# Linear attention with a butterfly feed-forward layer: keys of two batches biased by a maximum on VectorE, their sums on GpSimd, first slots and low parts in another order

## Chip, cores and metric

The kernel runs on one core of a Trainium2 chip. The metric is the device time of one execution in microseconds (us); of several runs the median is taken.

## What is computed

The input `x` is 4 batches of 1024 tokens with 128 channels. The layer is post-norm linear attention followed by a post-norm feed-forward layer. Cut to what matters:

```python
q, k, v = split(x @ W_qkv)                     # 16 heads of 64
q = relu(q @ W_f + b_f)
k = relu(k @ W_f + b_f)
kv = einsum('bhnd,bhne->bhde', k, v)
out = einsum('bhnd,bhde->bhne', q, kv)
k_sum = k.sum(axis=2)
normalizer = einsum('bhnd,bhd->bhn', q, k_sum)
out = out / (normalizer[..., None] + 1e-06)
x = layernorm(x + out @ W_out + b_out)
h = butterfly(x @ W_exp + b_exp, up_weights)   # 9 stages over 512 features
h = butterfly(gelu(h + up_bias), down_weights)
x = layernorm(x + h @ W_con + b_con + down_bias)
```

## The kernel before, in words

**Folding.** `W_f` is multiplied into the query and key weights once (`fold_wf`), `W_out` into the value weights (`fold_vo`), and both butterflies into the feed-forward weights: the up one on GpSimd (`up_step`), the down one on VectorE in nine `down_step` calls. Matrices that feed TensorE as fp32r are kept as a high and a low part; one such product is three matmuls (`split`, line 516). ScalarE writes a high part, VectorE subtracts it from the source to get the low part (`lo`, line 960).

**Slots.** All four compute engines run the same loop of 48 slots, each engine with its own instructions in program order. Nothing but semaphores and the order in which the loop's body is written sets the order of work. Up to slot 4 a slot projects two tiles of 128 tokens to keys, later one tile (`k_tiles`, tile s + 4 in slot s, up to slot 27). Batch 2 has the tiles 16 to 23, batch 3 the tiles 24 to 31. From slot 4 on a slot also projects two of the 64 query steps. From slot 10 on VectorE normalises two query steps a slot (`normalise_q`, line 1061), splits them (`qn_lo`), and one slot later TensorE multiplies them by the head maps (`add_attn`).

**Keys.** A key half-tile (128 tokens by 512 columns) is three matmuls and a fourth one, `ones_r` by `bf_rows` (line 568), which adds the bias `b_f`. ScalarE takes it out of its bank with a ReLU (`k_relu`, line 806). VectorE adds each tile to `k_total` (`k_sum`, lines 1029 and 1033), and TensorE multiplies it by `x` into `kx_ps` (`add_kx`, line 588). ScalarE copies `kx_ps` out at the end of a batch (`kx_copy`), and the sum over the tokens is turned into `ksum_cols` by VectorE (`ksum_mask`, line 1039), in slots 6, 14, 22 and 30.

**Shared banks.** Three PSUM banks form a ring (`ring`) for keys, queries, norms and hidden tiles: a bank is written again when the use three places before it has been taken out. One more bank, `desk`, takes all transposes, the key sums and the head maps, one after another (`desk_of`, `take_desk`): the next use waits until the one before has been copied out. A low part that VectorE still has to make from `desk` therefore holds the next transpose on TensorE. The transposed `x` of a batch goes over `desk` in slots 2, 6, 10, 14, 18 and 22, with its low part made a slot later (`xT_lo`). The transposed attention output goes over it in slots 15, 19, 23, ... (`transpose_attn`), in the first half of TensorE's slot, and the feed-forward output in slots 22, 26, 30, 34, ... (`transpose_y`).

**Layer norms.** In slots 15, 19, 23, ... VectorE adds the residual and takes mean and variance (`add_x`), GpSimd computes the reciprocal root (`rstd_of`, lines 492 and 495), and VectorE ends the norm (`layer_norm_end`, line 1079). From slot 22 on the second norm does the same (`residual`).

**SP's queue.** SP issues the large loads in a fixed order. `load_down(8)`, the last coefficients of the down butterfly, stands behind `spread(0)`, which writes the first reciprocals to memory and reads them back spread over the partitions.

## Time and profile before

| what | value |
|---|---|
| median of 3 runs | 353.05 us (352.67 to 353.06) |
| the profiled execution's own time | 351.33 us |
| its span, first to last instruction | 349.4 us |
| TensorE (PE) busy | 321.5 us, 92% of the span |
| VectorE (DVE) busy | 227.2 us, 65% |
| ScalarE (ACT) busy | 165.5 us, 47% |
| GpSimd (POOL) busy | 77.6 us, 22% |
| mean granted TensorE clock | 0.99 |

A busy share is the time in which an engine works on an instruction. Matmuls are pipelined, so what a matmul costs in a dense stretch is the distance from its start to the next one's start, which is shorter than its duration. "PEld" is the weight load, which overlaps the matmuls. Behind a group stands, in brackets, how long its engine was idle just before it and what ended that.

### The profile page before, as it was taken

Reading aid. Unit: us, or ns where it says so; the run is one execution under the profiler, and the core shown is the slowest. Engines: PE = TensorE matmul, PEld = TensorE weight load, DVE = VectorE, ACT = ScalarE, POOL = GpSimd, SP = SyncE. Lnnn points to the kernel's source line nnn. Section 1 sums busy time; section 2 is a strip of 40 time slices with the busy share of each in tenths; the row PEclk is TensorE's granted clock in tenths of the full one; section 3 lists DMA queues with packets and bytes.
Section 4 is the critical chain, followed back from the end, with each engine's and each line's share of the span. In section 5 each row is a group of like instructions: output and inputs, shape, how many; then the busy total and the mean of one; then the engine's idle time right before and its main releaser. Section 6 shows DMA issues by size and latency. Waiting matters only on the chain.

```text
span 349.4 us, 5085 instructions
## 1 busy us (share of the span) xinstructions
PE 321.5 (92%) x1825; PEld 222.5 (64%) x1825; DVE 227.2 (65%) x471; ACT 165.5 (47%) x273; POOL 77.6 (22%) x77
## 2 busy tenths in 40 slices
PE   4998999999799999999999999999999799999870
PEld 3855677766477767677777677577777466455440
DVE  2534999984979577756632876458638826575643
ACT  3532345444446464565564646365656543233340
POOL 4079599950000001101000110011001102111211
PEclk9999999999999999999999999999999999999996
DMA  6992353826502800720081005600370092190021
GB/s 178 289 265 62 120 180 122 258 108 159 144 2 65 181 0 5 175 68 3 6 217 23 0 2 130 144 2 3 89 185 2 4 215 58 45 248 12 0 61 31
DMA packets 25602, 33.73 MB, mean 97 GB/s; under 512 B 4169, under 2 KB 14441, under 8 KB 25577
## 3 DMA queue, kind: packets, MB, share of 16 engines
q1 hardware_dynamic: 25416, 33.38, 36.2%
q8 instruction: 14, 0.23, 0.3%
q14 instruction: 12, 0.09, 0.1%
q10 hardware_dynamic: 160, 0.03, 0.0%
HBM read 31.04 MB, written 2.36 MB: 96 GB/s over the span
## 4 chain that ended last, share of the span: by engine, by line
PE 77%; DVE 10%; DMA 4%; SPq 2%; issue 2%; POOL 2%; ACT 1%; POOLq 0%; DVEq 0%; ACTq 0%
PE ring L516 27%; PE kx_ps L588 14%; PE attn_ps L516 8%; PE ring L684 7%; PE ring L608 4%; PE attn_ps L638 4%; PE desk L525 4%; PE ring L568 4%; DMA x<-_L_ffn_down_weights_dram 2%; PE desk L622 2%; PE desk L597 2%; DVE qn L1061 2%; DMA xs<-in_L_attn_x_dram 2%; DVE stats L1070 1%; SPq L419 1%
## 5 line engine op out<-in xcount | busy, mean ns | idle before, releaser
L813 ACT ACTIVATE q<-ring,bf_col 128x512 f32<-128x512 f32 x64 | 43.9, 689 | 51.9 <-PE ring L516 51.4
L588 PE MATMUL kx_ps<-k,xs 128*128 128x512 f32 x128 | 60.2, 592 | 0.8 <-ACT k L806 0.8
L492 POOL TENSOR_TENSOR var_eps<-mean_var,ln_eps 128x4 f32<-128x4 f32 x16 | 7.5, 467 | 235.0 <-DVE mean_var L1074 235.0
L806 ACT ACTIVATE k<-ring 128x512 f32<-128x512 f32 x64 | 38.3, 599 | 32.6 <-PE ring L568 32.4
L1061 DVE TENSOR_TENSOR qn<-q,recips 128x512 f32<-128x512 f32 x64 | 42.2, 698 | 3.3 <-DMA recips<-recip_rows 3.3
L960 DVE TENSOR_TENSOR qn_l<-qn,qn_h 128x512 fp32r<-128x512 f32 x48 | 32.1, 680 | 15.2 <-ACT qn_h L799 15.1
L484 POOL TENSOR_TENSOR y<-hid,y_up 128x512 f32<-128x512 f32 x18 | 34.5, 1941 | 20.0 <-DMA hid<-in_L_ffn_up_weights_dram 19.2
L799 ACT ACTIVATE qn_h<-qn 128x512 fp32r<-128x512 f32 x48 | 29.6, 628 | 17.0 <-DVE qn L1061 17.0
L588 PEld LDWEIGHTS kx_ps<-k,xs 128*128 128x128 f32 x128 | 24.1, 189 | 19.2 <-issue 16.5
L516 PE MATMUL ring<-xT_h,wq_h 128*128 128x512 f32 x64 | 35.7, 557 | 0.0
L1033 DVE TENSOR_TENSOR k_total<-k_total,k 128x1024 f32<-128x1024 f32 x24 | 33.4, 1390 | 0.8 <-ACT k L806 0.6
L516 PE MATMUL ring<-wk_h,xT_h 128*128 128x512 f32 x64 | 28.7, 448 | 0.9 <-DVE wk_l L960 0.9
L684 PE MATMUL ring<-hid,wdn 128*128 128x512 f32 x64 | 29.0, 595 | 0.0
L869 ACT ACTIVATE hid<-ring,bup_col 128x512 f32<-128x512 f32 x32 | 22.0, 687 | 10.5 <-PE ring L516 10.3
L516 PE MATMUL ring<-xT_h,wq_l 128*128 128x512 f32 x64 | 25.3, 395 | 0.0
L516 PE MATMUL ring<-wk_h,xT_l 128*128 128x512 f32 x64 | 25.2, 394 | 0.0
L516 PE MATMUL ring<-xT_l,wq_h 128*128 128x512 f32 x64 | 25.1, 392 | 0.0
L516 PE MATMUL ring<-wk_l,xT_h 128*128 128x512 f32 x64 | 25.1, 391 | 0.0
L568 PE MATMUL ring<-bf_rows,ones_r 128*128 128x512 f32 x64 | 25.0, 391 | 0.0
L516 PE MATMUL attn_ps<-qn_h,m_h 128*128 128x512 f32 x48 | 20.0, 417 | 3.6 <-DVE x L982 2.5
L684 PEld LDWEIGHTS ring<-hid,wdn 128*128 128x128 f32 x64 | 11.9, 190 | 13.0 <-issue 12.1
L876 ACT ACTIVATE late<-ring,bdn_col 128x512 f32<-128x512 f32 x8 | 5.5, 688 | 28.5 <-PE ring L684 28.5
(131 smaller groups left out, 555.7 us busy)
## 6 DMA issues: line engine op xcount, KB each, us to landing
recips<-recip_rows SPq DMA_DIRECT2D x64, 256.0 KB, 5.4
...
```

The lines of the kernel that those rows point to most:

```text
L484: g.tensor_tensor(term_up[f].rearrange("p (hi j lo) -> p hi j lo", j=2, lo=lo), w[:, :, :, :, f], yv[:, :, f:f + 1, :].to_broadcast([128, ...
L516: last = t_.matmul(dst, lhsT, rhs, start=start and n == 0, stop=stop and n == len(pairs) - 1)
L568: t_.matmul(dst, ones_r[:, :], bf_rows[:, :], start=False, stop=True).then_inc(s_made, 1)
L588: t_.matmul(kx_ps[half], xs[b % XBUF][:, t, :], k[kt % KRING][:, half * CH:(half + 1) * CH], start=t == 0, stop=t == TILES - 1).then_inc(s ...
L684: last = t_.matmul(bank(("down", n))[:, :], wdn[:, i, :], hid[:, i, :], start=i == 0, stop=i == HT - 1)
L799: a_.activation(dst, src, ACT.Copy).then_inc(done, 1)
L806: a_.activation(k[kt % KRING][:, half * CH:(half + 1) * CH], bank(("k", kt, half))[:, :], ACT.Relu).then_inc(s_taken, 1)
L813: a_.activation(q[:, i % QRING, :], bank(("q", i))[:, :], ACT.Relu, bias=bf_col[:, :])\
L869: a_.activation(hid[:, i, :], bank(("up", f))[:, :], ACT.Gelu, bias=bup_col[:, i:i + 1])\
L960: v.tensor_tensor(dst, src, high.bitcast(fp32), ALU.subtract).then_inc(done, 1)
L1033: v.tensor_tensor(k_total[:, :], k_total[:, :], k[kt % KRING][:, :], ALU.add).then_inc(s_ks, 1)
L1061: v.tensor_tensor(qn[:, a % NRING, :], q[:, a % QRING, :], recips[:, a % PAIRS // RC, a % RC, :], ALU.mult).then_inc(s_qn, 1)
```

## The change

The keys of batches 2 and 3 lose the bias matmul. Their half-tiles are taken out of the ring by VectorE as `max(z, -b)` in place of ScalarE's ReLU. Since `relu(z + b) = max(z, -b) + b`, the missing `b` is put back in sums: `kx` gets `b_f` times the sum of `x` over the tokens (`kx_end`, which needs `x_sum`, made with a new `reduce_sum` of 512 columns for each half of the transposed `x`), and `ksum_cols` gets 1024 times `b_f` (in `ksum_mask`). The 14 additions to `k_total` of these batches go from VectorE to GpSimd. Besides:

- Before the loop TensorE folds the key weights first and transposes all of the first batch's `x` afterwards. The fold of the query weights moves behind both key halves of the first tile. The wait for the bias rows moves to their first use.
- The three transposes over `desk` that stood together at the end of slot 1 go to slot 0 (`wcon`), slot 1 and slot 2 (`v`).
- The last two down steps no longer use `attn_ps` (`PS_LAST`), and the first `add_attn` waits for seven steps instead of nine.
- The low parts of the head maps (`m_lo`) are made a slot later on VectorE.
- The last reciprocal stands ahead of the layer norm of its slot (35).

```diff
+    PS_LAST = 7
+    BARE = 2 * TILES
-    desk_of = {("wq",): 0, ("v", 0): 1, ("v", 1): 2, ("wcon",): 3}
+    desk_of = {("wq",): 0, ("wcon",): 1, ("v", 0): 2, ("v", 1): 3}
+    WCON_SLOT = 0
+    V_SLOT = {1: 0, 2: 1}
...
@@ GpSimd, in each slot, behind rstd_of
+                for kt in kx_tiles(s):
+                    b, t = kt // TILES, kt % TILES
+                    if kt < BARE or t == 0:
+                        continue
+                    pool.wait_ge(s_ktaken, k_taken["k", kt, 1])
+                    if t == 1:
+                        pool.wait_ge(s_dmade, desk_of["ksum", b - 1] + 1)
+                        g.tensor_tensor(k_total[:, :], k[(kt - 1) % KRING][:, :], k[kt % KRING][:, :],
+                                        ALU.add).then_inc(s_ks, 1)
+                    else:
+                        k_summed(pool, b, t - 1)
+                        g.tensor_tensor(k_total[:, :], k_total[:, :], k[kt % KRING][:, :], ALU.add).then_inc(s_ks, 1)
...
@@ TensorE, project_k
+                if kt >= BARE:
+                    split(dst, (xT_h[:, b % 2, tok], xT_l[:, b % 2, tok]), (wk_h[:, cols], wk_l[:, cols]))\
+                        .then_inc(s_made, 1)
+                    return
...
@@ TensorE, add_attn
-                    pe.wait_ge(s_dn, 3 * STAGES)
+                    pe.wait_ge(s_dn, 3 * PS_LAST)
...
@@ VectorE
+            def k_max(kt, half):
+                dve.wait_ge(s_made, ring_of["k", kt, half] + 1)
+                if half == 0:
+                    if kt == BARE:
+                        dve.wait_ge(s_bfm, 2)
+                    dve.wait_ge(s_kxt, 2 * (kt - KRING) + 2)
+                    k_summed(dve, (kt - KRING) // TILES, (kt - KRING) % TILES)
+                v.tensor_tensor(k[kt % KRING][:, half * CH:(half + 1) * CH].rearrange("p (h d) -> p h d", d=D),
+                                bank(("k", kt, half))[:, :].rearrange("p (h d) -> p h d", d=D),
+                                bf_minus[:, :].rearrange("p (o d) -> p o d", o=1).to_broadcast([128, CH // D, D]),
+                                ALU.max).then_inc(s_ktaken, 1)
...
             def xT_lo(b, c):
                 dve.wait_ge(s_xTh, CHUNKS * b + c + 1)
+                if TILES * b >= BARE:
+                    v.reduce_sum(x_part[:, b, c:c + 1], desk[:, :], axis=mybir.AxisListType.X).then_inc(s_xpart, 1)
                 lo(xT_l[:, b % 2, c * CH:(c + 1) * CH], desk[:, :], xT_h[:, b % 2, c * CH:(c + 1) * CH], s_dtaken)
...
+                if s in KX_SLOT and TILES * KX_SLOT[s] >= BARE:
+                    kx_end(KX_SLOT[s])
+                for kt in k_tiles(s)[:1]:
+                    if kt >= BARE:
+                        k_max(kt, 0)
...
+                if s - 1 in MAPS_SLOT and STEPS * MAPS_SLOT[s - 1][0] < WHOLE:
+                    m_lo(*MAPS_SLOT[s - 1])
...
+                for kt in k_tiles(s)[:1]:
+                    if kt >= BARE:
+                        k_max(kt, 1)
+                if s in LATE_NORM_SLOT:
+                    reciprocal(LATE_NORM_SLOT[s])
```

**Order, first place.** TensorE from the start to the first `add_kx` (line 588 before, 634 now). `ring<-ident,q` are transposes of weights, `kx_ps<-ident,xs` transposes of `x`, `wf_diag` the folds. Before:

```order
L525 MATMUL kx_ps<-ident,xs 128x128 [waits xs_0_loaded]
L525 MATMUL kx_ps<-ident,xs 128x128 x3
L543 MATMUL attn_ps<-wf_diag,q 128x128 [waits wT_copied_act,wf_loaded]
L543 MATMUL attn_ps<-wf_diag,q 128x128 x3
L543 MATMUL spare_ps<-wf_diag,q 128x128 [waits wT_copied_dve]
L543 MATMUL spare_ps<-wf_diag,q 128x128 x3
L525 MATMUL kx_ps<-ident,xs 128x128 x4
```

Now:

```order
L583 MATMUL attn_ps<-wf_diag,q 128x128 [waits wT_copied_act,wf_loaded]
L583 MATMUL attn_ps<-wf_diag,q 128x128 x3
L583 MATMUL spare_ps<-wf_diag,q 128x128 [waits wT_copied_dve]
L583 MATMUL spare_ps<-wf_diag,q 128x128 x3
L565 MATMUL kx_ps<-ident,xs 128x128 [waits xs_0_loaded]
L565 MATMUL kx_ps<-ident,xs 128x128 x7
```

The folds no longer stand behind the transposes that wait for the load of `x`.

**Order, second place.** VectorE in slot 22 and the head of slot 23, from the mask of the third batch's key sums. Before:

```order
L1039 TENSOR_TENSOR ksum_cols<-head_mask,desk 128x256 [waits ring_bank_made,desk_made]
L1061 TENSOR_TENSOR qn<-q,recips 128x512 [waits qn_lo,qn_hi,recips_of_pairs_0_loaded]
L1061 TENSOR_TENSOR qn<-q,recips 128x512 [waits qn_lo,qn_hi]
L1029 TENSOR_TENSOR k_total<-k 128x1024 [waits desk_made,ring_bank_taken]
L960 TENSOR_TENSOR qn_l<-qn,qn_h 128x512 [waits qn_hi]
L1095 TENSOR_TENSOR y<-desk,x 128x512 [waits desk_made]
...
L1061 TENSOR_TENSOR qn<-q,recips 128x512 [waits qn_lo,qn_hi,recips_of_pairs_2_loaded]
L1061 TENSOR_TENSOR qn<-q,recips 128x512 [waits qn_lo,qn_hi]
L960 TENSOR_TENSOR xT_l<-desk,xT_h 128x512 [waits xT_hi]
```

Now:

```order
L1114 SCALAR_TENSOR_TENSOR ksum_cols<-desk,bf_times,head_mask 128x256 [waits ring_bank_made,desk_made]
L1081 TENSOR_TENSOR k<-ring,bf_minus 128x512 [waits k_summed,kx_half_added,ring_bank_made]
L1141 TENSOR_TENSOR qn<-q,recips 128x512 [waits qn_lo,qn_hi,recips_of_pairs_0_loaded]
L1141 TENSOR_TENSOR qn<-q,recips 128x512 [waits qn_lo,qn_hi]
L1009 TENSOR_TENSOR qn_l<-qn,qn_h 128x512 [waits qn_hi]
L1081 TENSOR_TENSOR k<-ring,bf_minus 128x512 [waits ring_bank_made]
L1175 TENSOR_TENSOR y<-desk,x 128x512 [waits desk_made]
...
L1081 TENSOR_TENSOR k<-ring,bf_minus 128x512 [waits k_summed,kx_half_added,ring_bank_made]
L1141 TENSOR_TENSOR qn<-q,recips 128x512 [waits qn_lo,qn_hi,recips_of_pairs_2_loaded]
L1141 TENSOR_TENSOR qn<-q,recips 128x512 [waits qn_lo,qn_hi]
L1183 TENSOR_REDUCE x_part<-desk 128x1 [waits xT_hi]
L1009 TENSOR_TENSOR xT_l<-desk,xT_h 128x512
```

A key half-tile now stands at the head of each slot, in front of the normalisations, and a reduction in front of the low part that frees `desk`.

**Order, third place.** GpSimd in the slots 20 to 24 of the changed kernel, where before it had only the pairs of lines 492 and 495:

```order
L544 TENSOR_TENSOR k_total<-k 128x1024 [waits desk_made,ring_bank_of_bare_k_taken]
L520 TENSOR_TENSOR var_eps<-mean_var,ln_eps 128x4 [waits mean_var_0_done]
L523 TENSOR_TENSOR rstd<-var_eps,minus_half 128x4 [waits var_eps_0_done]
L548 TENSOR_TENSOR k_total<-k_total,k 128x1024 [waits k_summed,ring_bank_of_bare_k_taken] x3
L520 TENSOR_TENSOR var_eps<-mean_var,ln_eps 128x4 [waits mean_var_1_done]
```

The sum of slot 22 (first row) stands behind that slot's norm, the sum of slot 23 behind the norm of slot 23, and the next two follow at once.

## Rows read from the trace of the kernel before

**Rows 1.** The page, busy time and 40 slices of the span.
```profile
PE 321.5 (92%) x1825; PEld 222.5 (64%) x1825; DVE 227.2 (65%) x471; ACT 165.5 (47%) x273; POOL 77.6 (22%) x77
PE   4998999999799999999999999999999799999870
```
**Rows 2.** The page, chain that ended last, shares by engine.
```profile
PE 77%; DVE 10%; DMA 4%; SPq 2%; issue 2%; POOL 2%; ACT 1%; POOLq 0%; DVEq 0%; ACTq 0%
```
**Rows 3.** TensorE in order of time, slot 25: start us, us, engine, line, operation.
```profile
215.36 0.39 PE L516 MATMUL ring<-wk_h,xT_l 128*128 128x512 f32 x1
215.60 0.39 PE L568 MATMUL ring<-bf_rows,ones_r 128*128 128x512 f32 x1
```
**Rows 4.** Groups of instructions: busy, mean ns of one, idle before.
```profile
L1033 DVE TENSOR_TENSOR k_total<-k_total,k 128x1024 f32<-128x1024 f32 x24 | 33.4, 1390 | 0.8 <-ACT k L806 0.6
L1086 DVE TENSOR_TENSOR x<-desk,xs 128x512 f32<-128x512 f32 x8 | 5.5, 686 | 6.9 <-PE desk L525 6.9
L826 ACT ACTIVATE kx<-kx_ps 128x1024 f32<-128x1024 f32 x4 | 4.1, 1024 | 0.0
```
**Rows 5.** TensorE in order of time, start to slot 0.
```profile
7.90 1.92 PE L543 MATMUL attn_ps<-wf_diag,q 128*128 128x128 f32 x8
11.32 0.75 PE L525 MATMUL kx_ps<-ident,xs 128*128 128x128 f32 x4
13.81 0.47 PE L516 MATMUL ring<-wk_h,xT_h 128*128 128x512 f32 x1 [0.87 <-DVE wk_l L960]
14.81 1.05 PE L543 MATMUL attn_ps<-wf_diag,q 128*128 128x128 f32 x8
18.45 1.96 PE L588 MATMUL kx_ps<-k,xs 128*128 128x512 f32 x4 [0.78 <-ACT k L806]
```
**Rows 6.** ScalarE in order of time: the copy that the first fold waits for.
```profile
4.78 0.60 ACT L879 ACTIVATE q<-ring 128x512 f32<-128x512 f32 x1 [1.08 <-PE ring L525]
```
**Rows 7.** TensorE in order of time, the transposes at the end of slot 1.
```profile
29.23 0.60 PE L525 MATMUL desk<-ident,q 128*128 128x128 f32 x4
32.47 0.48 PE L516 MATMUL ring<-wk_h,xT_h 128*128 128x512 f32 x1
```
**Rows 8.** The chain in order of time, and TensorE and VectorE around slot 11.
```profile
85.61 7.31 DMA x<-_L_ffn_down_weights_dram
95.07 0.47 PE L516 MATMUL attn_ps<-qn_h,m_h 128*128 128x512 f32 x1 [2.53 <-DVE x L982]
100.67 1.09 PE L622 MATMUL desk<-vo,kx 128*64 128x128 f32 x16
```
**Rows 9.** GpSimd and VectorE in order of time, alone and side by side.
```profile
32.06 1.28 POOL L488 TENSOR_TENSOR y_up<-y 128x512 f32<-128x512 f32 x1
33.49 1.52 POOL L484 TENSOR_TENSOR y<-hid,y_up 128x512 f32<-128x512 f32 x1
33.55 2.33 DVE L978 TENSOR_TENSOR late<-x,recips 128x512 f32<-128x512 f32 x1
76.94 1.16 DVE L1033 TENSOR_TENSOR k_total<-k_total,k 128x1024 f32<-128x1024 f32 x1
```
**Rows 10.** VectorE in order of time, slots 22 to 24.
```profile
190.09 0.42 DVE L1039 TENSOR_TENSOR ksum_cols<-head_mask,desk 128x256 f32<-128x256 f32 x1 [7.99 <-PE desk L597]
190.43 1.28 DVE L1061 TENSOR_TENSOR qn<-q,recips 128x512 f32<-128x512 f32 x2
197.14 1.12 DVE L1079 TENSOR_SCALAR y<-y,mean_var,rstd 128x128 f32<-128x128 f32 x4 [1.18 <-POOL rstd L495]
199.38 0.68 DVE L960 TENSOR_TENSOR xT_l<-desk,xT_h 128x512 fp32r<-128x512 f32 x1
```
**Rows 11.** TensorE in order of time, slot 23.
```profile
200.12 0.66 PE L525 MATMUL desk<-ident,late 128*128 128x128 f32 x4 [0.63 <-DVE xT_l L960]
```

**Rows 12.** Windows: stretch, length, then busy of PE, PEld, DVE, ACT, POOL, clock, DMA share, GB/s.
```profile
190.00:207.00 17.00, 16.37 (x91) 11.73 (x94) 14.39 (x41) 9.84 (x16) 3.13 (x4) 1.00 0.00 1
```

More of the change, by code:

```diff
@@ L152, in postln_linear_attention_butterfly_ffn_kernel @@
             ring_of[use] = len(ring_of)
-    desk_of = {("wq",): 0, ("v", 0): 1, ("v", 1): 2, ("wcon",): 3}
+    BARE = 2 * TILES
+    k_taken, taken = {}, {}
+    for use in ring_of:
+        if use[0] == "k" and use[1] >= BARE:
+            k_taken[use] = len(k_taken) + 1
+        else:
+            taken[use] = len(taken) + 1
+    ring_use = {n: use for use, n in ring_of.items()}
+    desk_of = {("wq",): 0, ("wcon",): 1, ("v", 0): 2, ("v", 1): 3}
+    WCON_SLOT = 0
+    V_SLOT = {1: 0, 2: 1}
     for s in range(SLOTS):
@@ L346, in bank, with emptied @@
             return ring[ring_of[use] % 3]
+        def emptied(eng, use):
+            if use in k_taken:
+                eng.wait_ge(s_ktaken, k_taken[use])
+            else:
+                eng.wait_ge(s_taken, taken[use])
         def k_summed(eng, b, t):
@@ L895, in _ @@
             for s in range(SLOTS):
-                if s in KX_SLOT:
+                if s in KX_SLOT and TILES * KX_SLOT[s] < BARE:
                     kx_copy(KX_SLOT[s])
                 for kt in k_tiles(s)[:1]:
-                    k_relu(kt, 0)
+                    if kt < BARE:
+                        k_relu(kt, 0)
                 if s in NORM_SLOT:
                     norm_eps(NORM_SLOT[s])
-                if s == 0:
-                    for half, fold in enumerate([attn_ps, spare_ps]):
-                        act.wait_ge(s_fold, half + 3)
-                        hi(wq_h[:, half * CH:(half + 1) * CH], fold[:, :], s_wh)
                 if s >= NO_KEYS:
@@ L916, in _ @@
                 for kt in k_tiles(s)[:1]:
-                    k_relu(kt, 1)
+                    if kt < BARE:
+                        k_relu(kt, 1)
                 for a in split_spreads(s)[1:]:
                     qn_hi(a)
+                if s == 0:
+                    for half, fold in enumerate([attn_ps, spare_ps]):
+                        act.wait_ge(s_fold, half + 3)
+                        hi(wq_h[:, half * CH:(half + 1) * CH], fold[:, :], s_wh)
                 for n in range(ALLCH):
@@ L1116, in _ @@
                 lo(wk_l[:, cols], fold[:, :], wk_h[:, cols], s_wl)
+            dve.wait_ge(s_xTh, 1)
+            lo(xT_l[:, 0, 0:CH], kx_ps[0], xT_h[:, 0, 0:CH], s_xTl)
             dve.wait_ge(s_bfh, 2)
@@ L1147, in _ @@
                 for kt in kx_tiles(s):
[L1148 removed]
+                    if kt % TILES and kt < BARE:
                         k_sum(kt)
@@ L1162, in _ @@
                     layer_norm_end(0, ATT_T_SLOT[s], x1[:, ATT_T_SLOT[s] % X1BUF, :, :], s_x1)
[L1163 to L1166 removed]
                 if s in YT_SLOT:
                     layer_norm_end(1, YT_SLOT[s], y[:, YT_SLOT[s] % 2, :, :], s_yo)
[L1169 to L1173 removed]
+                if s in V_SLOT:
+                    dve.wait_ge(s_dmade, desk_of["v", V_SLOT[s]] + 1)
+                    v.tensor_copy(wT[:, (4 + V_SLOT[s]) * CH:(5 + V_SLOT[s]) * CH], desk[:, :]).then_inc(s_dtaken, 1)
+                if s == WCON_SLOT:
                     dve.wait_ge(s_dmade, desk_of["wcon",] + 1)
```

91 lines of the change are left out of this document (53 added, 38 removed).

## The prediction

> **What bounds the kernel now.** I read the page first. TensorE is busy in 92% of the span, and 33 of its 40 slices stand at 9 [rows 1]. In the chain that ended last TensorE has 77% and VectorE 10% [rows 2]. So what the change takes from TensorE's queue counts in full, as long as its three suppliers keep up, and a wait that it puts in front of TensorE counts in full too. Then I read TensorE, VectorE and GpSimd in order of time at the places which the change touches. The sum below is made against the profiled execution (351.33 us, span 349.4 us), the median of the runs is 1.7 us above it (353.05 us), and I carry the difference over to the median. A measurement of this kernel can tell about 0.2%, 0.7 us, from no change.
>
> **The bias matmuls.** 32 of them go (16 tiles by 2 halves). The matmul of line 568 starts 0.24 us behind the one before it, against a duration of 0.39 us [rows 3]. I take 0.23 us, the distance that repeats in most of the dense stretches: 32 x 0.23 = 7.4 us off TensorE. All of it lies on the path: **-7.4 us**.
>
> **Start.** Before, the folds of the key weights begin at 7.90 us, behind the transposes of x. What they need is ScalarE's copy, which ends at 4.78 + 0.60 = 5.38 us [rows 6]. So they can begin at 5.5. Two folds took 11.32 - 7.90 = 3.4 us [rows 5], to 8.9; eight transposes of x follow. At this stage instructions go at half the later pace: a fold of 8 records took 1.71 us from start to start, and 1.05 us in all from 14.81 on [rows 5]. The eight transposes take 1.7 us at the slow pace, to 10.6. ScalarE and VectorE need some 0.7 us each for the high and low part, so the first key matmul starts at 11.5 in place of 13.81 [rows 5]. Behind it come two key halves (0.93 us each, with about 0.1 us for the bias rows that are late), the two folds of the query weights (0.9 us each) and the first `add_kx`: at 15.1 in place of 18.45 [rows 5], with the wait of 0.78 us in front of it gone, because the folds now cover the ReLU. That is **-3.4 us**. Bounds: -1.5 if the second half's copies run late, -4.5 if the fast pace comes earlier too. The granted clock shows 1.00 through this stretch, although the durations halve behind 11.3 us. By the Trainium skill, "TensorE: Matmul & The Clock Gate", TensorE starts at 1.2 GHz and rises to 2.4 GHz when it has been kept busy; the durations agree, the clock column here doesn't show it.
>
> **Transposes of slot 1.** The next matmul starts 32.47 - 29.23 = 3.2 us behind the first of three transposes, which are 0.44 us of work each [rows 7]. The rest is waiting for VectorE to clear `desk`. Spread over three slots, each finds it free: 3.2 - 3 x 0.44 = 1.9, **-1.9 us**. VectorE's chain of down steps then starts earlier too, by more than TensorE gains, so it isn't what is late next.
>
> **Slot 11.** TensorE waits 2.53 us for the last down step, whose coefficients need 7.31 us from issue, behind the first reciprocals on SP's queue [rows 8]. With seven steps awaited this goes: **-2.5 us**. VectorE still stands in its queue at that load: at 85.61 - 5.3 + 7.3 = 87.6 us, with the two steps before, and works on till 91. Behind it stands the low part of x (now with a reduction, 0.69 us by the nearest PSUM row [rows 4]), which frees `desk` at about 93.7; TensorE wants it for the head maps 5.6 us into its slot [rows 8], at 92.8. So **+0.9 us** (bounds 0 and 2.5).
>
> **Where VectorE becomes tied to TensorE.** By instructions it loses 14 sums of 1.16 us alone [rows 9] (1.39 us in the mean [rows 4]) and gets 32 maxima. They read PSUM and one SBUF row; the nearest row is 0.69 us for 512 columns from PSUM [rows 4], about 0.63 us from start to start. Sum: 32 x 0.63 - 14 x 1.15 = +4 us, with 4 reductions (2.6 us) and 2 `kx_end` of about 1.15 us (ScalarE needed 1.02 [rows 4]) +9 us over 140 us. ScalarE loses 32 ReLUs that nobody waited for: no gain. That is affordable in the mean. The order matters more. Each slot's first VectorE instruction now waits for TensorE's first key half of the same slot. Behind it stand two normalisations (1.28 us together [rows 10]), the reduction and the low part of x (1.3 us), and this frees `desk` for the transpose of the attention output, which TensorE reaches three groups of 0.7 us into the slot. In slots 15, 19 and 23: VectorE is done at 0.9 + 0.65 + 1.2 + 1.3 = 4.05 us, TensorE is there at 2.1, so it stands for 2.0 us. Before, VectorE wasn't tied and the wait was nothing in slot 19, about 0.25 us in slot 15 and 0.63 in slot 23 [rows 11]. Slot 15: **+1.7**, slot 19: **+2.0**. Slot 23 is read from [rows 10]: mask at 190.09, end of the norm of slot 22 at 198.2 (8.1 us later), low part at 200.0. With two maxima for one sum that norm ends about 8.2 us after the mask, then maximum, two normalisations, reduction, low part, and up to 0.7 us in which GpSimd's sum blocks them: 12.0. TensorE, without two bias matmuls, is there at 8.9: 3.1 in place of 0.6, **+2.4 us**. Together **+6.1** (bounds +2 and +9).
>
> **GpSimd's sums against VectorE.** One sum has 1024 columns. 512 took 1.28 us alone [rows 9], so I take 2.5. The rows also show what happens side by side: GpSimd's product ran 33.49 to 35.01, VectorE's, issued at 33.55, ended at 35.88 [rows 9]; 35.88 - 35.01 = 0.87, its own length. So it stood until GpSimd was done. By the Trainium skill, "SBUF — State Buffer", § SBUF: two separate sides, the pair of ports is "an exclusive lock, not a bandwidth split", taken by a VectorE instruction with two SBUF inputs or a GpSimd one for its whole length. By that rule and by the row alike a sum costs up to 2.5 us of VectorE; if the two only slowed each other, the cost below would be half. The maxima read PSUM and one SBUF tensor, so they don't stand. Mostly a sum is released by the second maximum, runs under the end of the slot and blocks nobody that is late. Behind a norm it waits, then two run nearly back to back over the next slot's normalisations: 16 and 17 (TensorE stands 0.5 more), 24 (VectorE is 4 us late and has 5 us of slack through the ring, 0), 28 (the low part of the maps holds `desk`, 1.0), 26 (the maps a slot on, 0.5). **+2.0 us** (bounds 0 and 14 x 2.5 = 35 on VectorE, of which half might reach TensorE).
>
> **Rest.** The reciprocal of slot 35 costs nothing and gains nothing: the load it starts is awaited three slots later. The end chain of the last norm is untouched.
>
> **Sum.** -7.4 - 3.4 - 1.9 - 2.5 + 0.9 + 6.1 + 2.0 = **-6.2 us**: 345.1 profiled, 353.05 - 6.2 = **346.9 us** for the median.
>
> **Rivals.**
> - *VectorE doesn't hold TensorE* (0.17). It would have to reach `desk` in time in 15, 19 and 23. For it speaks that TensorE waits only 0.63 us there now [rows 11]; against it the order of instructions, in which four stand behind a TensorE result. Without 6.1 and 2.0: 353.05 - 14.3 = 338.8 us; with half of them 342.9.
> - *GpSimd's sums take the gain* (0.14, slower). The mechanism is the lock, its place the slots 14 to 28, its price up to 2.5 us a sum. VectorE is busy 14.4 of the 17 us of the slots 22 and 23 already [rows 12]. If half of 35 us reached TensorE, 17.5 in place of 2.0: +9.3, 362.3 us. It decides from 6.2 + 2.0 = 8.2 us on, that is 0.6 us a sum. Against it: a slot has about 8.5 us, a sum 2.5, and the ring gives a late maximum some 5 us.
> - *The start gives nothing* (0.07). Loads and copies, not the order, set the first slots: without 3.4 and 1.9 the sum is -0.9, 352.1 us, at the edge of what can be told.
>
> **How the numbers follow.** The forecast (343 to 351.5) has 0.62. The range, 340 to 353, holds it, the half-way case of the first rival and the third. Left out are the full first rival and most of the second. Faster: 0.62 + 0.17 and most of the third, 0.82 in all; within 0.7 us 0.05; slower 0.13.
>
> **What would show it.** Right: no row of the bias matmul behind slot 11; first key matmul near 11.5 us and first `add_kx` near 15.1; the 2.53 us wait gone; three waits of 2 to 3 us of the attention transposes for `xT_l`; normalisations of 2 to 3 us beside GpSimd's sums of about 2.5. Wrong: sums of 4 us or more with VectorE rows stretched in most slots and TensorE at 8 tenths from 120 to 260 us; or no waits there at all.

## The result, and the profile after

The changed kernel takes 359.38 us (median of 4 runs, 358.34 to 359.59) against 352.86 us (352.52 to 353.06) of the kernel before, run beside it: a ratio of 1.018, interval 1.0158 to 1.0202. Forecast were 346.9 us and the range 340 to 353. The time went the other way, and past the range.

The page of the changed kernel: busy time, the 40 slices of TensorE and its clock, and the chain that ended last.

```profile
PE 317.7 (89%) x1793; PEld 217.1 (61%) x1793; DVE 260.8 (73%) x497; ACT 145.1 (41%) x241; POOL 114.0 (32%) x91
PE   5899799999999798879899498998899799989980
PEclk9999999999999999999999789999999999999998
PE 51%; DVE 26%; POOL 7%; issue 5%; DMA 5%; SPq 3%; ACT 2%; POOLq 0%; DVEq 0%; ACTq 0%
```

Against [rows 1] TensorE has 3.8 us less work and the span is 8.4 us longer. Its share of the chain fell from 77% [rows 2] to 51%; VectorE went from 10% to 26% and GpSimd from 2% to 7%. So TensorE now waits, and what it waits for leads to VectorE and from there to GpSimd. The digit 4 in TensorE's row, with the 7 and 8 in the clock's, is one place around 200 us.

TensorE's waits over the whole kernel (what it waited for, us in total, times, longest), the four that matter:

```profile
PE desk L565 <- DVE xT_l L1009: 8.3, 3, 4.7
PE ring L556 <- DVE k L1081: 3.3, 3, 1.5
PE desk L565 <- DVE m_l L1009: 2.2, 2, 1.7
PE desk L565 <- DVE q L1261: 2.0, 1, 2.0
```

The first line was predicted: three waits of the attention transposes for the low part of `x`, in slots 15, 19 and 23, 7.1 us in all. The rows in order of time give 1.80, 1.80 and 4.68 us. The second line was not predicted: TensorE finds its ring bank still full because a maximum is late. The third is for the low parts of the head maps, the fourth for the copy of the value weights in slot 2.

VectorE's and GpSimd's groups of instructions (busy, mean ns of one, idle before) show what is behind it:

```profile
L1141 DVE TENSOR_TENSOR qn<-q,recips 128x512 f32<-128x512 f32 x64 | 46.9, 771 | 4.2 <-DMA recips<-recip_rows 4.2
L1159 DVE TENSOR_SCALAR x<-x,mean_var,rstd 128x128 f32<-128x128 f32 x32 | 23.4, 791 | 8.3 <-POOL rstd L523 8.3
L1081 DVE TENSOR_TENSOR k<-ring,bf_minus 128x512 f32<-128x512 f32 x32 | 21.9, 683 | 17.9 <-PE ring L556 17.8
L1159 DVE TENSOR_SCALAR y<-y,mean_var,rstd 128x128 f32<-128x128 f32 x32 | 13.1, 470 | 9.1 <-POOL rstd L523 9.1
L548 POOL TENSOR_TENSOR k_total<-k_total,k 128x1024 f32<-128x1024 f32 x12 | 29.8, 2487 | 7.2 <-DVE k L1081 6.7
```

The scalings that end a norm, which do exactly what they did before, took 343 ns each there and take 791 (`x`) and 470 ns (`y`) now: 23.4 + 13.1 - 17.8 = 18.7 us more of VectorE. The normalised queries went from 42.2 to 46.9 us. The maxima are 683 ns each, as estimated, and a sum is 2.49 us, as estimated. Order of time at slots 22 to 24 (start, us, engine, line) shows how the scalings get longer; in the kernel before the same four took 1.12 us [rows 10].

```profile
196.38 1.02 POOL L523 TENSOR_TENSOR rstd<-var_eps,minus_half 128x4 f32<-128x4 f32 x1
197.37 2.38 POOL L544 TENSOR_TENSOR k_total<-k 128x1024 f32<-128x1024 f32 x1
197.43 3.17 DVE L1159 TENSOR_SCALAR y<-y,mean_var,rstd 128x128 f32<-128x128 f32 x4 [1.19 <-POOL rstd L523]
200.53 0.68 DVE L1081 TENSOR_TENSOR k<-ring,bf_minus 128x512 f32<-128x512 f32 x1
202.93 0.68 DVE L1009 TENSOR_TENSOR xT_l<-desk,xT_h 128x512 fp32r<-128x512 f32 x1
203.66 1.11 PE L565 MATMUL desk<-ident,late 128*128 128x128 f32 x4 [4.68 <-DVE xT_l L1009]
...
210.41 4.98 POOL L548 TENSOR_TENSOR k_total<-k_total,k 128x1024 f32<-128x1024 f32 x2
210.47 5.25 DVE L1159 TENSOR_SCALAR x<-x,mean_var,rstd 128x128 f32<-128x128 f32 x4 [1.19 <-POOL rstd L523]
215.64 0.68 DVE L1081 TENSOR_TENSOR k<-ring,bf_minus 128x512 f32<-128x512 f32 x1
216.38 0.51 PE L556 MATMUL ring<-wk_h,xT_h 128*128 128x512 f32 x1 [1.48 <-DVE k L1081]
```

GpSimd's reciprocal root releases VectorE's scalings, and the next instruction in GpSimd's own queue is the sum. The scalings start 0.06 us behind the sum in slots 15, 22 and 23. The scalings end at 197.43 + 3.17 = 200.60, which is the sum's end, 199.75, and 0.85 us. Taken one by one (shortest, median and longest, in ns), the delay lies on a single one of the four:

```profile
L1159 DVE TENSOR_SCALAR y<-y,mean_var,rstd x4: 334/334/2401, 197.4 to 200.3; 128x128 f32<-128x128 f32 x4
```

The first, started at 197.43, ended at 199.83, 0.08 us behind the sum. So it stood until the sum was done (it was held, in the words used below), and the other three ran as fast as ever. With two sums in a row two of the four are held, 5.25 us in all. The maximum that frees the ring and the low part that frees `desk` stand behind the scalings in VectorE's queue.

The window of 200 to 210 us (length, then busy time of PE, PEld, DVE, ACT, POOL, clock, DMA share, GB/s) shows a second price of the 4.68 us stall: the granted clock is 0.66, and the matmuls behind the stall come 0.43 us apart in place of 0.23.

```profile
200.00:210.00 10.00, 6.34 (x18) 4.48 (x19) 7.31 (x21) 1.72 (x3) 1.14 (x2) 0.66 0.00 0
```

**Where the 8.4 us of span are.** I cut each profile where TensorE starts the key sums of slots 14 and 30. Every kernel that was run is in this table; what is between the two cuts is what the maxima and sums can reach, apart from slots 12 and 13. The runs other than the first two are explained below.

| kernel | median, us | span | to slot 14 | 14 to 30 | from 30 |
|---|---|---|---|---|---|
| before | 352.86 to 353.37 | 349.4 | 117.5 | 139.9 | 92.0 |
| changed | 359.38 | 357.8 | 113.1 | 153.2 | 91.5 |
| sum_first | 357.61 | 356.1 | 113.4 | 151.2 | 91.5 |
| sum_behind_scaling | 355.49 | 355.1 | 115.1 | 148.5 | 91.5 |
| sums_768 | 353.29 | 352.5 | 114.4 | 146.6 | 91.5 |
| sums_half | 348.92 | 346.4 | 111.7 | 143.2 | 91.5 |
| sums_tiny | 347.38 | 344.1 | 111.9 | 140.8 | 91.5 |
| sum_on_vector | 350.69 | 348.6 | 112.7 | 144.4 | 91.5 |
| max_later | 369.58 | 369.7 | 117.0 | 161.3 | 91.4 |
| changed_low_first | 361.25 | 357.8 | 111.4 | 155.1 | 91.3 |
| low_part_first | 346.86 | 346.9 | 113.0 | 142.7 | 91.2 |
| low_first_v_copy | 345.40 | 343.6 | 111.3 | 141.1 | 91.3 |
| order_only | 348.48 | 346.4 | 114.1 | 140.3 | 92.0 |
| v_copy_on_scalar | 348.81 | 345.5 | 113.7 | 140.3 | 91.5 |
| order_low_first | 345.52 | 343.4 | 112.5 | 138.9 | 92.0 |
| order_both | 344.74 | 341.4 | 111.3 | 138.9 | 91.2 |

The changed kernel wins 4.4 us up to slot 14 and loses 13.3 us in the next sixteen slots, although it issues 27 bias matmuls less in them. The column "to slot 14" differs by up to 3.4 us between kernels whose code is the same up to slot 12 (111.7 in `sums_half`, 115.1 in `sum_behind_scaling`), so I lean on the column "14 to 30", which is still one profile of each.

The medians have a scatter of their own. Each kernel was run beside the kernel before, whose median stayed within 352.86 and 353.37 us, but single executions of one kernel lie up to 4.6 us apart (`v_copy_on_scalar`), and most kernels have four or five. So a difference of 1 or 2 us between two medians can't be told from none.

Between the two cuts the stretch splits into TensorE's work and its standing still (start and end, length, then busy time of PE, PEld, DVE, ACT, POOL, clock, DMA share, GB/s). The changed kernel, the same with sums of one column (`sums_tiny`), and the new order without maxima (`order_only`):

```profile
113.07:266.30 153.23, 135.89 (x807) 94.02 (x806) 116.48 (x216) 59.12 (x100) 45.17 (x27) 0.98 0.25 57
111.87:252.63 140.76, 132.85 (x807) 92.94 (x805) 92.67 (x216) 59.17 (x100) 13.86 (x27) 1.00 0.30 67
114.13:254.44 140.31, 138.65 (x834) 98.17 (x833) 87.61 (x191) 77.21 (x129) 11.00 (x13) 1.00 0.28 65
```

Without the bias matmuls TensorE has 138.65 - 132.85 = 5.8 us less work, and it stands 7.9 us in place of 1.7. So the maxima alone gain nothing in these slots. The full sums add 9.4 us of standing, and 3.0 us of work, since the matmuls come further apart at a lower granted clock.

### The profile page after: what moved, and what is told of

The parts are those of the page before. It is cut to its first block, busy times and chain, and to the rows that moved or that the text cites. A ratio compares the mean times of both kernels' runs of the same rounds, so it can differ in the third digit from the quotient of the medians.

```text
span 357.8 us, 5029 instructions
## 1 busy us (share of the span) xinstructions
PE 317.7 (89%) x1793; PEld 217.1 (61%) x1793; DVE 260.8 (73%) x497; ACT 145.1 (41%) x241; POOL 114.0 (32%) x91
## 4 chain that ended last, share of the span: by engine, by line
PE 51%; DVE 26%; POOL 7%; issue 5%; DMA 5%; SPq 3%; ACT 2%; POOLq 0%; DVEq 0%; ACTq 0%
PE ring L556 19%; PE kx_ps L634 8%; PE ring L730 7%; DVE qn L1141 5%; PE attn_ps L684 4%; PE desk L565 3%; PE attn_ps L556 3%; DVE x L1159 3%; DVE stats L1150 3%; POOL k_total L548 3%; POOL rstd L523 3%; DVE k L1081 3%; DMA bf_col<-in_L_attn_b_f_dram 2%; DMA x<-_L_ffn_down_weights_dram 2%; DVE y L1159 2%
## 5 line engine op out<-in xcount | busy, mean ns | idle before, releaser
L1141 DVE TENSOR_TENSOR qn<-q,recips 128x512 f32<-128x512 f32 x64 | 46.9, 771 | 4.2 <-DMA recips<-recip_rows 4.2
L1081 DVE TENSOR_TENSOR k<-ring,bf_minus 128x512 f32<-128x512 f32 x32 | 21.9, 683 | 17.9 <-PE ring L556 17.8
L556 PE MATMUL ring<-wk_h,xT_h 128*128 128x512 f32 x64 | 29.8, 465 | 3.3 <-DVE k L1081 3.3
L548 POOL TENSOR_TENSOR k_total<-k_total,k 128x1024 f32<-128x1024 f32 x12 | 29.8, 2487 | 7.2 <-DVE k L1081 6.7
L1159 DVE TENSOR_SCALAR x<-x,mean_var,rstd 128x128 f32<-128x128 f32 x32 | 23.4, 791 | 8.3 <-POOL rstd L523 8.3
L851 ACT ACTIVATE k<-ring 128x512 f32<-128x512 f32 x32 | 19.1, 598 | 19.2 <-PE ring L614 19.2
L565 PE MATMUL desk<-ident,late 128*128 128x128 f32 x64 | 10.5, 288 | 12.5 <-DVE xT_l L1009 8.3
```

The source lines that it names most:

```text
L548: g.tensor_tensor(k_total[:, :], k_total[:, :], k[kt % KRING][:, :], ALU.add).then_inc(s_ks, 1)
L556: last = t_.matmul(dst, lhsT, rhs, start=start and n == 0, stop=stop and n == len(pairs) - 1)
L1081: v.tensor_tensor(k[kt % KRING][:, half * CH:(half + 1) * CH].rearrange("p (h d) -> p h d", d=D), bank(("k", kt, half))[:, :].rearrange("p ...
L1141: v.tensor_tensor(qn[:, a % NRING, :], q[:, a % QRING, :], recips[:, a % PAIRS // RC, a % RC, :], ALU.mult).then_inc(s_qn, 1)
L1159: ins = v.tensor_scalar(dst[:, t, :], dst[:, t, :], mean_var[i][:, t, 0:1], rstd[i][:, t:t + 1], ALU.subtract, ALU.mult)
```

## The experiments

The theory from these rows, A: the sums on GpSimd hold VectorE's scalings, and TensorE pays. B: VectorE is tied to TensorE by the first maximum of each slot. C: VectorE has too much work of its own. In the recorded expectations "lock" means that one of the two engines stands until the other's instruction is done.

A fourth, that GpSimd is simply too busy and hands things over late, falls by the waits of GpSimd and VectorE in the changed kernel. In front of the norms' first instruction GpSimd had always been idle, and the maxima waited for TensorE alone, 17.8 of 17.9 us:

```profile
POOL var_eps L520 <- DVE mean_var L1154: 164.0, 16, 24.3
DVE k L1081 <- PE ring L556: 17.8, 9, 6.9
```

### sum_first, sum_on_vector, order_only

`sum_first` changes the order of GpSimd's instructions in a slot, `sum_on_vector` gives the sums back to VectorE, `order_only` takes maxima and sums out and keeps the rest.

```diff
@@ sum_first, GpSimd, in each slot
-                if s in ATT_T_SLOT:
-                    rstd_of(0, ATT_T_SLOT[s])
-                if s in YT_SLOT:
-                    rstd_of(1, YT_SLOT[s])
                 for kt in kx_tiles(s):
...
+                if s in ATT_T_SLOT:
+                    rstd_of(0, ATT_T_SLOT[s])
+                if s in YT_SLOT:
+                    rstd_of(1, YT_SLOT[s])
@@ sum_on_vector, VectorE (and the loop over kx_tiles(s) leaves GpSimd)
-                    if kt % TILES and kt < BARE:
+                    if kt % TILES:
@@ order_only
-    BARE = 2 * TILES
+    BARE = BATCH * TILES
```

Expected of `sum_first`:

> GpSimd adds the key tile ahead of the reciprocal root in each slot, in place of behind it. Theory A (a sum that stands behind the root is released together with VectorE's scaling at the end of the norm, and the two lock each other out): the 64 scalings fall from 36.5 us busy to near the 17.8 us of the kernel before, the waits of TensorE for desk shrink, and the time falls by some 12 us, to 345 to 350 us. Rival B (VectorE is tied to TensorE by the first maximum of the slot and by the reduction): scalings get short, but the time stays at 355 us or more. Rival C (VectorE simply has too much work of its own): as B.

Expected of `sum_on_vector`:

> The 14 sums of batches 2 and 3 go back to VectorE; the maxima stay on it. Theory A: no lock is left, scalings and normalisations have the durations of the kernel before, but VectorE has 16 us more of its own; 349 to 354 us. Rival B: the tie and the reduction stay, and the sums come on top: 356 to 362 us. Rival C (own work): slower than the changed kernel's 359.4 us.

Expected of `order_only`:

> All keys keep the bias matmul, ScalarE's ReLU and VectorE's sums; only the reordering of the first slots, the seven awaited down steps, the low parts a slot on and the last reciprocal stay. In the changed kernel TensorE is 1.3 us ahead of the kernel before at the first norm and 3.5 us ahead at the second, ahead of any maximum. Theory A, B and C alike: 3 to 4 us faster than the kernel before, 349 to 350 us, unless the low parts a slot on cost something further down.

Measured: 357.61 us (354.81 to 357.9), ratio 1.0122 [1.0078, 1.0166]; 350.69 us (350.26 to 351.35), 0.994 [0.9917, 0.9962]; 348.48 us (347.43 to 350.29), 0.9891 [0.9846, 0.9935]. Giving the sums back to VectorE, which is the busier engine, wins 8.7 us. VectorE's groups in `sum_on_vector` and the waits of its TensorE:

```profile
L1129 DVE TENSOR_TENSOR qn<-q,recips 128x512 f32<-128x512 f32 x64 | 41.1, 680 | 4.6 <-DMA recips<-recip_rows 4.6
L1147 DVE TENSOR_SCALAR x<-x,mean_var,rstd 128x128 f32<-128x128 f32 x32 | 8.9, 341 | 8.3 <-POOL rstd L523 8.3
...
PE desk L553 <- DVE xT_l L997: 7.1, 3, 3.5
```

The scalings are back at 341 ns, and the waits for `xT_l` are 7.1 us, what the prediction said they would be. So neither B nor C explains the loss, and A stands. The tie is real all the same: `sum_on_vector` is not faster than `order_only`, which has 32 matmuls more. `sum_first` missed what A expected of it (345 to 350 us). Whenever the sum comes first, the root behind it is late instead: in slot 15 the scalings took 1.11 us again, but started at 133.59 in place of 131.04 us, and where the sum is late it still meets them (`x` 533 ns each, `y` 468). The ring is free in time, but TensorE's waits for `xT_l` grow from 8.3 to 11.1 us. Order on GpSimd does not remove the collision.

### max_later

If TensorE waits because four instructions stand behind the first maximum, take the maximum back behind them:

```diff
@@ VectorE, in each slot
-                for kt in k_tiles(s)[:1]:
-                    if kt >= BARE:
-                        k_max(kt, 0)
...
                 if s - 1 in X1T_SLOT:
                     x1T_lo(X1T_SLOT[s - 1])
+                for kt in k_tiles(s)[:1]:
+                    if kt >= BARE:
+                        k_max(kt, 0)
```

> The first maximum of a slot goes on VectorE behind the normalisations and the low parts that free desk; all else as changed. Theory A: desk is freed 0.7 us and the wait for TensorE's first key half earlier in three slots; 2 to 4 us off, 355 to 358 us. Rival B: the tie is the cost; 10 us or more off, 349 us or less. Rival C: no change.

Measured: 369.58 us (368.55 to 371.52), 1.0486 [1.0444, 1.0527], outside all of them. The waits of its TensorE:

```profile
PE ring L556 <- DVE k L1081: 12.3, 4, 3.8
PE desk L565 <- DVE xT_l L1009: 4.5, 2, 3.9
```

`desk` is free earlier (4.5 in place of 8.3 us), and the ring takes more than that back, 12.3 in place of 3.3 us. Standing still is not the whole of it: between the two cuts TensorE stands only 1.6 us longer than in the changed kernel (19.0 against 17.3) and works 6.5 us longer on the same matmuls (142.4 against 135.9), at a mean granted clock of 0.94 against 0.98. The first maximum has to stand early: with three banks it is the ring that bites next.

### sums_tiny, sums_half, sums_768

The changed kernel with GpSimd's sums cut in length, `w` = 1, 512 and 768 columns (the rest of the sum is left out, every wait stays). The second of the two additions is shown, the first is cut alike:

```diff
@@ GpSimd
-                        g.tensor_tensor(k_total[:, :], k_total[:, :], k[kt % KRING][:, :], ALU.add).then_inc(s_ks, 1)
+                        g.tensor_tensor(k_total[:, 0:w], k_total[:, 0:w], k[kt % KRING][:, 0:w], ALU.add).then_inc(s_ks, 1)
```

> The changed kernel with GpSimd's 14 sums cut from 1024 columns to one column each, so most of the sum is left out; every wait and semaphore stays. Theory A (each sum locks VectorE out of SBUF and that is the changed kernel's loss): this must be at or below the 350.7 us of the run with the sums on VectorE, since neither engine does them: 345 to 350 us, scalings of the norms' ends back at 343 ns each. Theory B (the maxima's load and the wait for desk alone are the loss, the sums only share the blame): 354 to 358 us.

> The changed kernel with each of GpSimd's 14 sums cut to 512 of its 1024 columns (half of the sum is left out). Theory A, lock time adds up with the length of a sum: half way between the run with one column and the 359.4 us of the changed kernel, 352 to 355 us. A theory of thresholds (a sum hurts only if it runs into the norm's end, which a short one misses): within 1.5 us of the run with one column.

> The changed kernel with GpSimd's 14 sums over 768 of their 1024 columns (the rest of the sum is left out). Between slots 14 and 30 the changed kernel took 12.5 us longer than with one column, with 512 columns 2.4 us. If the loss goes with the length of a sum, a straight line between those two gives some 7.4 us: 353 to 355 us. If it is a collision that decides (one sum pair in slot 22 that holds the norm's end until TensorE has emptied), then it is either near 349.5 us or near 358 us, and not between.

Measured: 347.38 us (345.38 to 349.17), 0.982 [0.9754, 0.9886]; 348.92 us (348.17 to 350.24), 0.9878 [0.9823, 0.9932]; 353.29 us (351.06 to 354.83), 0.9994 [0.9965, 1.0022]. VectorE's scalings of `x` in the three, in that order, each in a profile of its own:

```profile
L1159 DVE TENSOR_SCALAR x<-x,mean_var,rstd 128x128 f32<-128x128 f32 x32 | 8.9, 342 | 8.3 <-POOL rstd L523 8.3
```

```profile
L1159 DVE TENSOR_SCALAR x<-x,mean_var,rstd 128x128 f32<-128x128 f32 x32 | 15.6, 550 | 8.3 <-POOL rstd L523 8.3
```

```profile
L1159 DVE TENSOR_SCALAR x<-x,mean_var,rstd 128x128 f32<-128x128 f32 x32 | 19.5, 671 | 8.3 <-POOL rstd L523 8.3
```

The cost of the sums, everything else in place, is 359.38 - 347.38 = 12.0 us, with an uncertainty of some 2.5 us by the two intervals. It isn't one collision, since it grows with each step, and over the whole length it isn't a straight line. Count what VectorE is held beyond the run with one column, in both kinds of scalings and the normalised queries: 10.6 us with 512 columns, 17.1 with 768, 24.4 with 1024. The medians are 1.5, 5.9 and 12.0 us longer. From step to step that is (5.9 - 1.5) / (17.1 - 10.6) = 0.7 and 6.1 / 7.3 = 0.8 us of time for each held microsecond, and for the first 10.6 us held only 1.5 / 10.6 = 0.14. Between the two cuts it is 2.4, 5.8 and 12.4 us, that is 0.2, 0.5 and 0.9 for each held microsecond. Both say that the first microseconds are cheap and the later ones dear; where the bend is, four lengths don't show. `sums_half` missed its straight line (352 to 355 us) and came out at the edge of the theory of thresholds (1.54 us above one column, where up to 1.5 was expected). `sums_768` fell into the 353 to 355 us of a straight line between 512 and 1024 columns.

### sum_behind_scaling

Does it matter which of VectorE's instructions is held?

```diff
@@ GpSimd, ahead of each sum
                     pool.wait_ge(s_ktaken, k_taken["k", kt, 1])
+                    if s in ATT_T_SLOT:
+                        pool.wait_ge(s_x1, ATT_T_SLOT[s] + 1)
+                    if s in YT_SLOT:
+                        pool.wait_ge(s_yo, YT_SLOT[s] + 1)
```

> The changed kernel with its full sums on GpSimd, but in a slot that ends a norm GpSimd's sum also waits until VectorE's last scaling of that norm is done. Theory A1 (the loss is what a sum does to the scalings, which stand ahead of the next slot's first maximum): scalings back at 343 ns each, 350 to 352 us, near sum_on_vector. Theory A2 (a sum takes the same time from whatever VectorE does next in SBUF): the normalised q and the low parts get longer instead, 355 to 360 us.

Measured: 355.49 us (353.82 to 356.93), 1.0064 [1.0031, 1.0097]. Its groups and, in order of time, the place after the scalings of slot 23:

```profile
L1145 DVE TENSOR_TENSOR qn<-q,recips 128x512 f32<-128x512 f32 x64 | 58.3, 948 | 4.1 <-DMA recips<-recip_rows 4.1
L1163 DVE TENSOR_SCALAR x<-x,mean_var,rstd 128x128 f32<-128x128 f32 x32 | 8.9, 342 | 8.3 <-POOL rstd L523 8.3
...
212.27 5.19 POOL L552 TENSOR_TENSOR k_total<-k_total,k 128x1024 f32<-128x1024 f32 x2 [1.29 <-issue]
212.64 0.69 DVE L1085 TENSOR_TENSOR k<-ring,bf_minus 128x512 f32<-128x512 f32 x1 [0.50 <-PE ring L560]
213.25 4.77 DVE L1145 TENSOR_TENSOR qn<-q,recips 128x512 f32<-128x512 f32 x2
```

The scalings are back at 342 ns, and the normalised queries went from 41.2 us (one column) to 58.3. The maximum, which ran while the first of the two sums did, took its usual 0.69 us: it reads PSUM and one SBUF row. So A2: the sum takes its time from the next instruction of VectorE that it can hold, here one with two SBUF inputs. Moving it wins 3.9 us. No maximum is late for TensorE any more (3.3 us of waits for the ring before, none now), but the waits for `xT_l` stay, 8.9 us, and so do 8.1 us of the cost.

### changed_low_first, low_part_first, order_low_first

The low part of `x`, which frees `desk`, right behind the first maximum; the reduction over the tokens then reads the two halves in SBUF, later in the slot. In the changed kernel, in `sum_on_vector`, in `order_only` (which has no such reduction, so that there only the low part moves):

```diff
@@ VectorE
             def xT_lo(b, c):
                 dve.wait_ge(s_xTh, CHUNKS * b + c + 1)
-                if TILES * b >= BARE:
-                    v.reduce_sum(x_part[:, b, c:c + 1], desk[:, :], axis=mybir.AxisListType.X).then_inc(s_xpart, 1)
...
@@ VectorE, in each slot
+                if s - 1 in XT_SLOT:
+                    xT_lo(*XT_SLOT[s - 1])
                 for a in spreads(s)[:1]:
                     normalise_q(a)
...
-                if s - 1 in XT_SLOT:
-                    xT_lo(*XT_SLOT[s - 1])
...
+                if s - 1 in XT_SLOT:
+                    x_summed(*XT_SLOT[s - 1])
```

> The changed kernel with its full sums on GpSimd, and only the low part of the x map moved right behind the first maximum (the reduction then reads SBUF later in the slot). Theory A (the scalings held by a sum stand ahead of everything in the next slot, so the low part comes late wherever it stands in it): 354 to 357 us, the longest wait for xT_l still over 2 us. Rival (the low part's place alone is the trouble and GpSimd only makes it visible): 347 to 350 us, as without GpSimd's sums.

> Sums on VectorE as in sum_on_vector (350.69 us), and the low part of the x map moved on VectorE from behind the normalised q and the reciprocal to the place right behind the first maximum; the reduction over the tokens no longer reads desk but the two halves in SBUF, later in the slot. Theory A (desk is given back too late by VectorE, 7.1 us of waits for xT_l): the waits for xT_l fall below 2 us and the time to 344 to 347 us, below the 348.5 us of order_only. Rival C (the wait only moves to what VectorE now does later, the normalised q or the ring): 350 to 353 us.

> order_only (no maxima, 348.48 us) with the low part of the x map moved ahead in its slot in the same way. TensorE waits for xT_l there for only 1.3 us in two places, so theory A expects 347.5 to 348.5 us, and then low_part_first (346.86 us) is faster by the maxima themselves. If instead this run is at or below 346.9 us, the maxima are worth nothing in any order tried and only the moved low part gained.

Measured: 361.25 us (359.6 to 363.1), 1.0231 [1.0184, 1.0279]; 346.86 us (345.71 to 348.68), 0.9812 [0.9756, 0.9868]; 345.52 us (345.13 to 347.34), 0.98 [0.9754, 0.9847]. With the sums on VectorE the move wins 3.8 us; the waits for `xT_l` fall from 7.1 to 1.8 us. In the changed kernel it wins nothing, 4 us above what A expected, and the rival's 347 to 350 us are out: the waits for `xT_l` fall to 2.9 us, in one place, those for the ring rise from 3.3 to 8.2. And without maxima it wins 3.0 us, where at most 1.0 was expected. 1.4 us of that lie between slots 14 and 30; the rest lies before slot 14, where profiles of the same code differ by more. So `low_part_first` is not faster by the maxima; if either gained, it was the moved low part.

### v_copy_on_scalar, low_first_v_copy, order_both

The two copies of the value weights out of `desk` (slots 1 and 2) go to ScalarE, in `order_only`, in `low_part_first` and in `order_low_first`.

```diff
@@ ScalarE, in each slot, behind k_relu (and out of VectorE's slot)
+                if s in V_SLOT:
+                    act.wait_ge(s_dmade, desk_of["v", V_SLOT[s]] + 1)
+                    a_.activation(wT[:, (4 + V_SLOT[s]) * CH:(5 + V_SLOT[s]) * CH], desk[:, :], ACT.Copy)\
+                        .then_inc(s_dtaken, 1)
```

The reason is these rows of `order_only`, in order of time. Two sums of VectorE stand beside GpSimd's butterfly steps and take 4.77 us; the copy that frees `desk` stands behind them, and TensorE waits.

```profile
31.10 4.77 DVE L1107 TENSOR_TENSOR k_total<-k_total,k 128x1024 f32<-128x1024 f32 x2
35.80 0.68 DVE L1261 COPY q<-desk 128x512 f32<-128x512 f32 x1
36.53 0.66 PE L565 MATMUL desk<-ident,xs 128*128 128x128 f32 x4 [1.92 <-DVE q L1261]
```

> order_only (348.48 us: the new order, no maxima) with the two copies of the value weights out of desk moved from VectorE, where the second stands behind two sums and 1.9 us of wait follow in slot 3, to ScalarE. Theory D (the start does give its 3.3 us and that wait, with the matmuls at 0.63 us behind it, spends 2 of them): 345.5 to 347 us, the key sum of slot 6 at 58.2 to 58.8 us on TensorE in place of 60.1. Rival: the down steps or the wout load end the early slots anyway, and it stays at 348 to 349 us.

> low_part_first (346.86 us) with the copies of the value weights on ScalarE too. The run v_copy_on_scalar won 3.2 us up to the key sum of slot 6 and lost all but 0.4 us of it by slot 14, to a wait in slot 11 and before. If that holds here: 346 to 347 us, no gain outside the measurement. If the maxima's slots can use the early time: 344 to 345 us.

> The new order without the maxima, with the low part moved ahead (order_low_first, 345.52 us) and the value weights' copies on ScalarE. Beside low_first_v_copy (345.40 us) it has only the 32 bias matmuls back on TensorE and the maxima off VectorE. If the maxima are worth nothing once desk is free in time: 344 to 346 us. If they are worth the matmuls that they remove, it is slower than low_first_v_copy by over 2 us.

Measured: 348.81 us (345.88 to 350.45), 0.9853 [0.9781, 0.9925]; 345.40 us (344.94 to 347.95), 0.9793 [0.9748, 0.9838]; 344.74 us (343.16 to 345.62), 0.9767 [0.9729, 0.9805]. The wait is gone in all three, and the key sum of slot 6 starts at 56.9, 56.6 and 56.3 us, where the other twelve profiles with the new start have 57.8 to 61.9. Alone this brings nothing that can be told (348.81 against 348.48, four executions from 345.88 to 350.45), so theory D missed in the time and was right about the place. In the profile the next wait takes a part of it back, in slot 11 of `v_copy_on_scalar`:

```profile
89.81 1.29 DVE L1031 TENSOR_TENSOR late<-x,spare_ps 128x512 f32<-128x512 f32 x2 [3.79 <-DMA x<-_L_ffn_down_weights_dram]
94.55 0.67 DVE L1013 TENSOR_TENSOR xT_l<-desk,xT_h 128x512 fp32r<-128x512 f32 x1
95.27 1.09 PE L668 MATMUL desk<-vo,kx 128*64 128x128 f32 x16 [1.88 <-DVE xT_l L1013]
```

VectorE stands at the coefficients' load, and the low part behind two normalisations. With the low part moved ahead (`order_both`) the same wait is 0.50 us:

```profile
92.37 0.67 DVE L1013 TENSOR_TENSOR xT_l<-desk,xT_h 128x512 fp32r<-128x512 f32 x1
93.10 1.10 PE L668 MATMUL desk<-vo,kx 128*64 128x128 f32 x16 [0.50 <-DVE xT_l L1013]
```

`order_both` has the whole new order and no maxima. It has the lowest median, 2.3% below the kernel before and 4.1% below the changed one (344.74 / 359.38), though `order_low_first` and `low_first_v_copy` can't be told from it. `low_first_v_copy`, the same with maxima, is not faster: between the two cuts it takes 141.1 us against 138.9, where TensorE has 4.8 us less work and stands 7.0 us longer. The 32 matmuls that the maxima save gained nothing in any order tried.

## Why the prediction was wrong

**The step that failed** is "GpSimd's sums against VectorE", +2.0 us. It measured 12.0 us (`sums_tiny` against the changed kernel), 0.86 us a sum. The price of one sum was right (2.5 us assumed, 2.39 and 2.49 measured), the lock was right, and so was that the maxima get past it. What failed is the list of who stands in its way. The prediction looked for instructions with two SBUF inputs, found the normalised queries, and put five places at 0 to 1.0 us. It left out the scalings of the norm's end, one input in SBUF and a result in SBUF. They pay most, 18.7 of the 24.4 us that VectorE is held, and they can't miss the sum, as the root that releases them and the sum are neighbours in GpSimd's queue. The order of instructions on GpSimd showed that, and so did [rows 10], where the scalings wait for `rstd`.

By the Trainium skill, "SBUF — State Buffer", § SBUF: two separate sides, the shared ports are taken by a VectorE instruction "in a 2-port perf mode" too, not only by one with two SBUF inputs, and "VectorE: DVE Perf Modes", § Mode 2×_2P, puts scalar operations on fp32 in SBUF under such a mode. The trace agrees that they are held: 3.17 us for four that take 1.12 alone [rows 10]. That they run in such a mode no row here shows. The prediction drew on the half of the rule about two inputs.

The sentence that a sum mostly "runs under the end of the slot and blocks nobody that is late" was right for the first of the held time only: 10.6 us held cost 1.5, 24.4 cost 12.0. The prediction had no number for the room on VectorE and charged as if it were larger.

One reading was loose without consequence. The 0.87 us that VectorE's product in [rows 9] needed behind GpSimd's were called its own length; the shortest of its kind took 1.07 us. A held instruction ends sooner behind the other engine's than its own length, as the scaling above, 0.08 us behind the sum where it takes 0.33. Nor can a measurement of this kernel tell 0.2% from no change: single executions of the kernel before went from 351.37 to 355.94 us. The half-way time of the first rival is 342.8 us, not 342.9, and slot 23's difference 2.5, not 2.4.

**The rival that happened** is "GpSimd's sums take the gain", at 0.14 and 362.3 us. Its threshold was 0.6 us a sum, and 0.86 was measured. Half of what VectorE is held reached TensorE, as it assumed (12.0 of 24.4 us), but 24.4 us were held and not 35.

**The other terms.** Without the sums' cost the forecast was 346.9 - 2.0 = 344.9; `sums_tiny` took 347.38, so 2.5 us are left.
- *Bias matmuls and the tie of VectorE to TensorE*, -7.4 and +6.1, together -1.3: right, as far as can be told. `sums_tiny` is 1.1 us below `order_only`, inside what the two runs scatter. The two sizes fit too: 5.8 us less work and 6.2 us more standing between the two cuts. The waits were predicted at 1.95, 2.0 and 3.1 us in slots 15, 19 and 23; they are 1.79, 1.79 and 2.62 in `sums_tiny`, and 4.68 in slot 23 with full sums.
- *Start*, -3.4, and *transposes of slot 1*, -1.9: too large. The first `add_kx` came at 16.82 us against the 15.1 forecast, as the query weights' load held TensorE 1.18 us at 11.85; in `order_only` it came at 15.19. But in either, by slot 6 only about 2 of the 5.3 us are left (61.53 before, 59.5 in the mean of twelve profiles). The sentence that failed is that spread over three slots each transpose finds `desk` free: the copy in slot 2 stands behind two sums of VectorE, 1.5 to 2.5 us of wait. With that copy on ScalarE slot 6 is 4.6 to 5.3 us earlier, near the 5.3 forecast.
- *Slot 11*, -2.5 + 0.9: right. The wait for the last down step is gone, and one of 0.71 us for the low part came, of 1.88 us when TensorE is earlier.

## What to carry to other kernels

Before work goes to GpSimd, list every VectorE instruction that can lie beside it, those with one SBUF input and an SBUF result too, and ask which event releases both. If one does, the collision is no matter of chance, and shifting the work on GpSimd may only change who pays, as in `sum_first` and `sum_behind_scaling`. Here work taken from TensorE was no gain, since its replacement tied the engine that frees TensorE's banks to TensorE's own result. In such a case, count the instructions between that tie and the next release of a bank, and put the releasing ones first.

## What the runs showed beyond that

- A held engine has free room and then doesn't: 10.6, 17.1 and 24.4 us held gave 1.5, 5.9 and 12.0 us. One measurement at half the size would have suggested the change is safe.
- A stall of TensorE can cost more than its length. Behind the 4.68 us that end at 203.66 the granted clock is 0.50 up to 207.0, the lower of its two levels, and matmuls come 0.43 us apart in place of 0.23. The same spacing came some 1.2 us behind the 1.92 us stall of `order_only` that ends at 36.53 (granted clock 0.68 from 36.5 to 40), but not behind the 1.97 us one of the changed kernel that ends at 38.21 (1.00 from 38.2 to 42). What decides between the last two stays open.
- The same lock is in the early slots, between VectorE's own sums and GpSimd's butterfly steps: 4.77 us for two in `order_only`, 1.16 us for one alone [rows 9]. In slot 2 it decides when `desk` is free.
